# Another order for the end of the first layer's routing, in a two-layer transformer kernel on one Trainium2 core

## The reference, cut to what matters

```
gate_logits = xt @ Wg + bg
top_v, top_i = top_k(gate_logits, 2)
expert_label = one_hot(top_i, 8).sum(axis=1)
seq   = cumsum(expert_label, axis=0) * expert_label
valid = (seq > 0) & (seq <= 640)
flat_idx = where(valid, arange(8)[None, :] * 640 + (seq - 1), 8 * 640)
buf = zeros((8 * 640 + 1, d)).at[flat_idx].set(src)
disp = buf[:-1].reshape(8, 640, d)
h = silu(disp @ W1) * (disp @ W2);  out = h @ W3
```

## Time and profile before

| | |
|---|---|
| time, median of 3 runs (lowest, highest) | 849.43 us (849.05 to 851.46) |
| span of the profiled execution | 860.6 us |
| its own device time beside the span | not given; the span alone is 11.2 us above the median |
| PE, DVE, ACT, POOL busy | 93%, 71%, 50%, 46% |
| mean granted TensorE clock | 0.966 of full speed |
| DMA, mean | 58 GB/s |
| POOL's first and last send of layer 0 | 57.8 and 167.1 us |

### The profile page before, as it was taken

One profiled execution on the slowest core, in us unless ns is written; L12 is line 12 of the kernel. 1 busy time (PEld: TensorE's weight loads), 2 busy tenths in 40 slices (PEclk: granted clock), 3 DMA queues, 4 the chain that ended last, 5 costly groups with the idle time before them and its releaser, 6 DMA issues.

```text
span 860.6 us, 32362 instructions
## 1 busy us (share of the span) xinstructions
PE 798.8 (93%) x13678; PEld 695.9 (81%) x13678; DVE 611.5 (71%) x1776; ACT 434.6 (50%) x944; POOL 394.6 (46%) x399
## 2 busy tenths in 40 slices
PE   6999984489998799999999999999999999999998
PEld 5777764489997678888889888889888888878887
DVE  7897785357773676676677776787877778757865
ACT  6555533244542665656546566566574645523322
POOL 4357685604544473554645754556643533500000
PEclk9999996599998999999999999999999999999999
DMA  9824000163421200000010000100000000038661
GB/s 294 259 67 161 27 29 13 41 184 102 135 86 45 83 27 4 3 28 4 15 40 4 28 4 3 53 4 4 4 3 3 5 3 3 4 79 148 143 126 39
DMA packets 67904, 49.65 MB, mean 58 GB/s; under 512 B 5322, under 2 KB 62778, under 8 KB 67377
## 3 DMA queue, kind: packets, MB, share of 16 engines
q1 hardware_dynamic: 64288, 42.41, 18.4%
q0 software_dynamic: 3328, 5.16, 1.8%
q10 hardware_dynamic: 144, 0.02, 0.0%
HBM read 33.20 MB, written 16.10 MB: 57 GB/s over the span
## 4 chain that ended last, share of the span: by engine, by line
PE 72%; issue 13%; DVE 6%; DMA 3%; ACT 2%; another core or an unknown queue 1%; SPq 1%; POOL 1%; PEldq 0%; PEld 0%; DVEq 0%; ACTq 0%; POOLq 0%
PE psum L1560 11%; PE psum L1665 7%; PE psum L1716 6%; PE psum L1690 6%; PE psum L1244 6%; PE psum L2349 5%; PE psum L1595 5%; PE psum L1627 5%; PE psum L2367 4%; PE psum L1705 4%; PE psum L1607 3%; PE psum L1578 3%; PE psum L1279 3%; DMA sb_e_x<-disp 1%
## 5 line engine op out<-in xcount | busy, mean ns | idle before, releaser
L1560 PE MATMUL psum<-sb_wkv,sb_a_hs 128*128 128x512 f32 x384 | 122.1, 426 | 1.3 <-ACT sb_a_hs L2036 0.7
L2248 POOL TENSOR_TENSOR sb_a_qr<-sb_h,sb_a_csq 128x512 f32<-128x512 f32 x64 | 81.0, 1288 | 92.0 <-PE psum L1690 88.1
L2248 POOL TENSOR_TENSOR sb_a_qr<-sb_a_qp,sb_a_csq 128x512 f32<-128x512 f32 (+1 forms) x64 | 72.2, 1149 | 94.6 <-PE psum L1690 94.6
L1844 ACT ACTIVATE sb_a_vr<-sb_a_va,sb_consts 128x520 f32<-128x520 f32 x128 | 86.6, 726 | 14.6 <-DVE sb_a_va L2106 14.3
L310 POOL DMA_INDIRECT disp<-sb_h,sb_slot x64 | 67.9, 1062 | 32.2 <-issue 16.9
L1560 PEld LDWEIGHTS psum<-sb_wkv,sb_a_hs 128*128 128x128 f32 x384 | 63.6, 190 | 13.5 <-issue 1.2
L1183 POOL DMA_INDIRECT chosen<-sb_m_h3t,sb_e_row x40 | 39.4, 984 | 69.3 <-ACTq L1357 49.2
L1665 PE MATMUL psum<-sb_a_mid,sb_a_qr 64*64 64x65 f32 x2048 | 70.9, 218 | 0.0
L1244 PE MATMUL psum<-sb_e_xt,sb_e_ws 128*128 128x320 f32 x384 | 65.5, 327 | 5.4 <-issue 4.3
L1690 PE MATMUL psum<-sb_a_vr,sb_a_kb 64*64 64x130 f32 x1920 | 70.1, 272 | 0.0
L1244 PEld LDWEIGHTS psum<-sb_e_xt,sb_e_ws 128*128 128x128 f32 x384 | 59.6, 198 | 9.2 <-issue 5.2
(11 more groups left out here) (289 smaller groups left out, 1986.2 us busy)
## 6 DMA issues: line engine op xcount, KB each, us to landing
sb_h<-turned SPq DMA_DIRECT2D x32, 256.0 KB, 5.5
sb_e_w<-in_w SPq DMA_DIRECT2D x24, 256.0 KB
chosen<-sb_empty SPq DMA_DIRECT2D x8, 512.0 KB, 6.1
sb_a_g<-chosen SPq DMA_DIRECT2D x12, 256.0 KB, 3.1
disp<-sb_empty SPq DMA_DIRECT2D x4, 650.0 KB, 9.9
sb_e_x<-disp SPq DMA_DIRECT2D x7, 325.0 KB
sb_a_wo<-in_wo SPq DMA_DIRECT2D x4, 512.0 KB, 4.5
out<-sb_x SPq DMA_DIRECT2D x7, 256.0 KB, 3.9
```

What stands on the lines that cost most here:

```text
L1560: ins = pe.matmul(self.values_bank(i) if kv else self.bank[0], hs[:, part, at:at + P], self.Wkv[ws][:, h, w], start=(k == 0), stop=(k == 2))
L1844: ins = act.activation(self.Vr[i % 2][:, :, k, :], self.Va[i % 3][:], ACT.Copy, scale=self.c[("cos1", "sin1")[k]][:, n:n + 1])
L2248: ins = g.tensor_tensor(self.Qr[i % 2][:, k, :, t], qp, rows(self.csQ[:, k, c * P + t.start:(c + 1) * P], PH), ALU.mult)
```

## The change

Three orders are changed, and one split of a semaphore.

1. On DVE `last_root` and `input_means` of group 7 come ahead of `input_gated` and `route_labels` of group 6.
2. On PE `input_turned` of group 7 comes ahead of `queues_tensor` of group 6. On ACT `input_normed` of group 7 comes ahead of `mod_columns(1)`; it stays behind `input_kept` of group 6.
3. Group 6's slots are sorted like group 7's. POOL sends the four smaller slots of group 6, the four smaller of group 7, and then the eight larger ones, groups 6 and 7. The eight larger ones count on `dma_sent_high`; SP waits for 56 sends ahead of expert 0's rows and for 8 ahead of expert 1's.

```diff
+    ORDER = ([(c * G4 + n, k) for c in range(NGRP - 2) for n in range(G4) for k in range(2)]
+             + [(n, k) for k in range(2) for n in range(NT - 2 * G4, NT)])
+
     def dispatch(self, count, ready):
         g, S = self.pool, self.S
-        for _ in range(count):
-            c, rest = divmod(self.sent, 2 * G4)
+        for n, k in self.ORDER[self.sent:self.sent + count]:
+            c = n // G4
             if c > ready:
                 break
-            if rest == 0:
+            if n % G4 == 0 and k == 0:
                 g.wait_ge(S["r0_slot"], c + 1)
                 g.wait_ge(S["l0_H2"], c + 1)
-            last = c == NGRP - 1
-            k, n = divmod(rest, G4) if last else (rest % 2, rest // 2)
-            n += c * G4
+            late = c >= NGRP - 2 and k
...
-                bounds_check=self.slots_bound, oob_is_err=False).then_inc(S["dma_sent_high" if last and k else "dma_sent"], 16)
+                bounds_check=self.slots_bound, oob_is_err=False).then_inc(S["dma_sent_high" if late else "dma_sent"], 16)
...
         self.mod_tensor(1)
+        self.input_turned(NGRP - 1)
         self.queues_tensor(NGRP - 2)
-        self.input_turned(NGRP - 1)
         self.input_rows(NGRP - 1)
...
         self.input_kept(NGRP - 2)
+        self.input_normed(NGRP - 1)
         self.mod_columns(1)
-        self.input_normed(NGRP - 1)
         self.input_modulated(NGRP - 1)
...
-        if c < NGRP - 1:
+        if c < NGRP - 2:
             v.tensor_copy(self.slot[:, :, tiles], self.sf[:]).then_inc(S["r0_slot"], 1)
...
         self.input_stats(NGRP - 1)
+        self.last_root()
+        self.input_means(NGRP - 1)
         self.input_gated(NGRP - 2)
         self.route_labels(NGRP - 2)
-        self.last_root()
-        self.input_means(NGRP - 1)
         self.route_slots(NGRP - 2)
...
-        sp.wait_ge(S["dma_sent"], (2 * NT - G4) * 16)
+        sp.wait_ge(S["dma_sent"], (2 * NT - 2 * G4) * 16)
...
-        sp.wait_ge(S["dma_sent_high"], G4 * 16)
+        sp.wait_ge(S["dma_sent_high"], 2 * G4 * 16)
```

More of the change, by code:

```diff
@@ L1516, in l1_sync @@
                 sp.wait_ge(S["phase"], 4 + 3)
-                sp.wait_ge(S["dma_sent"], (2 * NT - G4 + 3) * 16)
+                sp.wait_ge(S["dma_sent"], (2 * NT - 2 * G4 + 3) * 16)
             for k in range(2):
```

## The result

In 20 runs of each on one chip the changed kernel took 852.07 us against 849.78 before; the ratio is 1.0039, with a 95% interval of 1.0023 to 1.0054, that is 3.3 us slower (1.9 to 4.6); the two medians lie 2.3 us apart. The forecast was 852.9, 3.5 us slower. A second chip, on which the kernel before took 860.5 us, gave 1.0064 (1.0041 to 1.0087), 5.5 us slower (3.5 to 7.5).

What follows compares the result with a forecast made beforehand. The landing of expert 2's rows, at the end of a full DMA queue behind POOL's last send, was taken to bound the kernel. Sends 5.1 us later less 1.65 us earlier start gave +3.5: 849.43 + 3.5 = 852.9 us, range 850.0 to 855.8.

Steps and rivals of the forecast that it cites:

- The last send, four sends later than the first of group 7: On POOL: 11 sends, not 7, from group 7's first to the last of all, 5.1 us more before expert 1's load.
- The full queue: SP's DMA queue, some 3.6 MB: expert 2's rows land at its end, 3.5 us later, at 187.8 us.
- PE's waits: PE waits 2.2 us for expert 1's rows and 4.8 us instead of 1.80 for expert 2's.
- S: On POOL: how much earlier group 7's first send, and so expert 0's load, comes; taken as 1.65 us.
- The clock: TensorE's clock may fall in PE's 4.8 us wait for expert 2's rows, costing 1.7 us more; not in the 3.5.
- Rival B: Loads behind POOL's last send: group 7 not earlier, or a fall of the clock; +5.1 to +5.3 us, 854.6; chance 0.25.
- D: Faster: expert 0's earlier start reaches the end, expert 2's rows landing by 180.9; 847.8 us; chance 0.1.
- The span: Profiled span 11.2 us above the timed median: most of the late completions were taken as absent from the timed runs.

Runs made afterwards that it cites:

- before, constants late: Kernel before, with layer 1's output weights, table, `wr` and `wd` (2.4 MB) issued behind expert 2's rows; ratios 0.9984 and 0.9996 to the kernel before.
- before, constants ahead of expert 0's rows: Kernel before, with layer 1's output weights, table, `wr` and `wd` issued ahead of SP's wait for the smaller slots; ratio 1.0051 to the kernel before.
- orders alone: Kernel before, with only the new orders on DVE, PE and ACT, POOL sending as before; ratio 1.0014 to the kernel before.
- sends alone: Kernel before, with only POOL's new order of sends, DVE, PE and ACT in the old order; ratio 1.0069 to the kernel before.
- changed, constants late: Changed kernel, with layer 1's output weights, table, `wr` and `wd` (2.4 MB) issued behind expert 2's rows; ratios 0.9999 and 0.9997 to the kernel before.
- changed, filled: Changed kernel, with one of group 6's larger slots sent in POOL's idle stretch ahead of group 7's smaller ones; ratio 1.0045 to the kernel before.
- changed, both edits: Changed kernel, with one larger slot of group 6 in POOL's idle stretch and layer 1's 2.4 MB behind expert 2's rows; ratios 0.9960 and 0.9967.

## Why the prediction was right, and what in it was not

The direction and the mechanism came out, and so did the size, the last in part by luck: a term that the sum left out and one that was probably too small work against each other. All profiles side by side, times in us, "statistics" being the start of their last instruction (L837 of before):

| kernel, profiles | slots of group 7 after statistics | expert 0's load after statistics | from it to expert 1's load | from expert 0's turning to expert 2's |
|---|---|---|---|---|
| before, 2 | 22.1, 18.9 | 28.4, 26.0 | 5.27, 5.03 | 17.6, 16.7 |
| before, constants late, 2 | 21.5, 20.7 | 27.8, 27.0 | 5.29, 5.18 | 15.9, 15.9 |
| before, constants ahead of expert 0's rows | 20.7 | 29.6 (behind the constants) | 6.54 | 14.6 |
| orders alone | 18.4 | 28.5 | 5.02 | 17.4 |
| sends alone | 21.3 | 27.8 | 10.15 | 21.5 |
| changed, 2 | 15.0, 19.3 | 21.5, 25.8 | 10.13, 10.14 | 21.9, 22.0 |
| changed, constants late, 2 | 15.6, 18.1 | 22.1, 24.7 | 10.12, 10.15 | 17.6, 19.2 |
| changed, filled | 19.2 | 25.8 | 8.85 | 20.7 |
| changed, both edits, 2 | 19.3, 15.1 | 25.8, 21.7 | 8.86, 8.86 | 16.1, 16.3 |

*The last send, four sends later than the first of group 7.* Forecast 10.4 us between the two loads where 5.3 were; measured 10.13. Right, and shown apart by the sends alone.

*The full queue.* Forecast: expert 2's landing keeps its distance to expert 1's load. Measured 14.3 for 15.1. That this landing sets the end is shown by the pair in one batch: 5.8 us by the ratios, 3.6 by the medians, for taking 2.4 MB out of its way.

*PE's waits.* Forecast 2.2 and 4.8; measured 3.38 and 3.84, and in the second profile 2.17 and 2.76. The near agreement of the first sums (7.0 and 7.2) is no proof: the second profile's is 4.9, with as long a way from turning to turning (22.0 and 21.9), as work at the lower clock stands in the place of waiting. That way is what counts. From expert 0's turning to expert 2's the change costs 21.95 - 17.15 = 4.8 us in the means of the two profiles each.

*S, how much earlier group 7's first send is: the term that was probably mis-sized.* I took 1.65 us. Expert 0's load came 27.3 us after the statistics in the mean of the four profiles of the old orders and sends that can be compared, and 23.9 in the seven with the new ones, which would make S 3.4. But the seven fall into two kinds. Three have next to no late completion (21.5, 22.1, 21.7); the other four have a mean of 25.5, which would make S 1.8, close to my 1.65. The step that failed is "I take it that most of this is not in them" of the late completions: they are in every profile with DVE's old order. Without them I had worked out slots of group 7 at 17.0 us before (152.7 - 135.7) and 15.4 after (151.1 - 135.7). For the new orders that is what the three clean profiles show (15.0, 15.6, 15.1). For DVE's old order there is no clean profile among six (18.9 to 22.1). Whether the new order makes clean executions more frequent, or these three were chance, is not shown, and the times put S at 2.6 or 0.4, with about 2 us either way. So the size of S stays open. What the new order can do is take the root out of the late stretch. In the second profile of the changed kernel the eleven instructions and the shift run through without a gap, and the stretch hits the labels of group 6 behind them. DVE's timeline:

```profile
136.35 0.16 DVE L954 SCALAR_TENSOR_TENSOR sb_l_y<-sb_l_t,sb_l_y 128x4 f32<-128x4 f32 x1
136.54 0.16 DVE L963 SCALAR_TENSOR_TENSOR sb_l_nm<-sb_l_mv,sb_l_y 128x4 f32<-128x4 f32 x1
...
142.91 0.17 DVE L983 CAST sb_rt_idx<-sb_rt_which 128x8 f32<-128x8 uint32 x1 [4.08 <-remote]
```

In the earlier trace rows the root itself lay in the stretch, and its last instruction began at 145.41.

*The clock.* I left it out of the sum and priced a fall at 1.7 us. It fell in both profiles of the changed kernel: 6.26 and 5.69 us for the down products, 4.63 without a fall, so 1.1 to 1.6. The Trainium skill ("TensorE: Matmul & The Clock Gate", "HAM oscillation — how this bites in real kernels") had said that a wait for data leaves the next batch slow; the traces agree here, 3.80 us without work and 1.63 us lost. After the waits of 1.80 and 2.50 in the two profiles of before nothing was lost (4.63 in both), but after 2.42 in the profile of the orders alone 1.0 was (5.62). It is the same with the waits for expert 1's rows: the clock fell behind 2.17, 2.33 and 2.82 us and not behind 3.38 and 3.06. In these rows the statement of the Trainium skill holds for some waits and not for others, and the length of the wait alone does not tell which.

*The sum anew:* 5.1 from the sends (4.8 as PE saw it), plus 1.4 for the clock, less S. With S = 3.4 that is 2.8 to 3.1, with 1.8 it is 4.4 to 4.7; measured 3.3 (1.9 to 4.6) on one chip and 5.5 (3.5 to 7.5) on the other. My 3.5 was 5.1 - 1.65, without the clock. Rival B's fall of the clock happened; its S = 0 is not what the profiles show, though the second chip's time does not exclude it. D did not happen: it needed the last send 1.8 us earlier than before, and expert 1's load came later, by 5.1 less S, 1.7 to 3.3 us. (By D's own landing of 180.9 it would have needed 3.4 us earlier, 184.29 - 180.9; the two figures of the prediction do not agree.)

*The span.* I read the 11.2 us by which the span stood above the median as the late stretch. But the chips differ by as much: the kernel before took about 849.5 us in two batches and 859.8 to 860.8 in three, on other chips, and spans are about 1.3 us below the times of their own executions (850.4 and 851.70 for the changed kernel's). The first profile's mean granted clock, 0.966, lies among those of the runs on the slower chips (0.960 to 0.976) and below every one of the kernel before in the 849.5 us batch of the last run (0.972 to 0.976). So nothing about that stretch can be read from the 11.2 us.

## What to carry to other kernels

When transfers are sorted so that the first consumer gets its part sooner, look at what waits for the last of them: here 5.1 us of sends went behind the early part, the 3.6 MB queue behind them started later, and the gain at the front was gone at the second consumer. Loads that nobody needs soon belong behind those that somebody waits for: this took back all that the change had cost (ratios 0.9999 and 0.9997). With the idle stretch filled as well, the kernel was 2.8 us faster than before; on the kernel before, late loads alone showed no gain that is clear of noise. And before an idle wait is counted as a gain, look whether the stretch ahead of it always has the same length.

## What the runs showed that I had not expected

Completions that come late, in the same stretch of some 9 us (136 to 145) behind the twelve small matmuls of `mod_tensor(1)`. On DVE its own previous instruction is done by its duration, and the release comes 0.2 to 1.4 us later, or up to 4.1 on "remote". ACT gets PE's matmuls late: in the earlier trace rows at 144.28 those modelled to end at 136.45. POOL keeps its pace of 1.28 us. A wait on "remote" on DVE or ACT is in that stretch in eight of the fourteen profiles. Three, all of the kernel before or with its loads moved, have only the short waits of DVE there. The last three, all with the new order, are the clean ones: two have no late release there, one has 0.8 us of it in all. A second such wait, of ACT for PE's last gates, comes in four profiles of the old order at 157 to 162 us (6.06 to 7.67 us). I did not look for the cause with a kernel of its own, and it stays open. Neither the lower clock nor the small matmuls bring it on alone: in the three clean profiles the twelve matmuls are there too, and the granted clock is 0.50 from 136 to 146 us.

Chips that ran the same kernel 1.3% apart (849.5 and 860.5 us). All ratios here are within a batch for that reason, and a difference between ratios of two batches is worth less than one within a batch.
